# The recurrence's skip made on VectorE and added on GpSimd, in place of four diagonal matmuls for each chunk

## The chip, the cores and the metric

The kernel runs on one core of a Trainium2 chip. The metric is the device time of one execution in microseconds. The engines run side by side and are ordered by semaphores alone: TensorE (PE in the profile, its weight loads PEld), VectorE (DVE), ScalarE (ACT), GpSimd (POOL) and the DMA queues. Everything is float32. A chunk is 128 tokens, a block is 512 tokens, that is four chunks.

## The reference, cut to what matters

The program has three stages on 4096 tokens of width 256. The first one is a graph product followed by a Mamba-2 block, the second a graph product followed by a Mamba-1 block, the third a mixture of experts. Only the first stage's recurrence is touched:

```python
xh, Bmat, Cmat = split(silu(conv(xBC)))          # xh: tokens x 8 heads x 64
xdt    = xh * dt[..., None]
Y_diag = einsum(Cc, Bc, Lmat, xdt)               # inside a chunk
Y_off  = einsum(Cc, prevs, exp(A_cum))           # from the carried state
Y = Y_diag + Y_off + xh * D[:, None]             # the last term is the skip
Y = Y * silu(z)
Y = Y * rsqrt(mean(Y * Y) + EPS) * norm_w
out = Y @ W_out @ W_lin + b_lin                  # W_out @ W_lin is made once ("Wc")
```

`D` has one number for each head. The kernel works in chunks of 128 tokens, which gives the same result.

## The kernel before

The first stage takes eight blocks, numbered 0 to 7. In the period of block b three kinds of work run side by side, and their order on every engine is one list written out by `order_a[b]`; a name in the list lets the generator of that name go one step.

- `product_a(b+2)` ("p" on TensorE, "w" on VectorE): the graph product of a later block. TensorE makes 64 matmuls of 512 columns (L685). Their weights are `exp(...)` of the adjacency matrix: ScalarE (L1659) and VectorE (L1146, L1153, pairs of 128x1024) work on them through six buffers `wgt`. In blocks 6 and 7 TensorE makes the next stage's first product instead (L709), which takes no VectorE work.
- `pre_a(b+1)`: norm, input projection, convolution (L1222, L1225) and silu of the next block. TensorE's step L745 waits for VectorE's L1201, the normalised input `xc`.
- `ssd(b)`: the recurrence. Chunk s has an `inner(s)` and an `outer(s)`. The order is inner(0), inner(1), outer(0), inner(2), outer(1), inner(3), outer(2), outer(3).

For one chunk, `inner(s)` transposes x on TensorE into the PSUM bank X (L785); VectorE makes `xdt` from it (L1251), copies B (L1254) and masks C times B (L1256); GpSimd makes `xdec` (L2190) and, when ScalarE has exponentiated E, multiplies E by the mask (L2195, called M(s) here). `outer(s)` is:

- TensorE: state's part Yo (L807, waits until the state of the chunk before, `hs`, is written by VectorE L1271), new state St (L812), then into bank Y the skip as four matmuls with a 128x128 diagonal matrix of D (L817), and on top of it eight matmuls of 64 columns, the chunk's own part (L823, waits for M(s)).
- GpSimd: `hd(s)`, the decayed state (L2207).
- VectorE: tmp = Yo times decay (L1266), the new state hs = hd + St (L1271), tmp = tmp + Y (L1275), z = tmp times z (L1278). ScalarE then squares z (L1660) into `ms`, and overwrites `tmp` with it, so L1266 of the next chunk waits for that.

After the fourth chunk ScalarE makes `rms`, VectorE scales the four chunks of z (L1288, L1292), and TensorE transposes them (L840, waits for each scaled chunk), multiplies by Wc (L849), and makes the block's norm (L634, L638) and message (L861).

The setup makes `diagD` (L1124) at the start of the program, and at the second pair of message blocks Wc by L875 on TensorE and L1320 on VectorE. `rows` holds three broadcast vectors that one DMA loads (L2127); ScalarE's first exponential waits for it.

Of the kernel before, what the change touches and what calls it, by code (L numbers as in the profile page):

```python
# [148 lines left out]
def build(nc, t):  # L149
    with ExitStack() as ctx:  # L150
# [7 lines left out]
        def sb(c, name, shape, dt=F32):  # L158
            return c.enter_context(nc.sbuf_tensor(name, shape, dt))
# [34 lines left out]
        rows = sb(cA, "rows", [128, NROW])  # L194
        Bbc, dtb, Abc = rows[:, 0:256], rows[:, 256:288], rows[:, 288:296]
        diagD = sb(cA, "diagD", [128, 4, 128])
# [22 lines left out]
        hd = sb(cA, "hd", [64, 512])  # L219
        cA.close()  # L220
# [53 lines left out]
        ring_a, ring_b = Ring(PS[2:5], 6 * NB // 2), Ring(PS[5:8], 6 * NB // 2 + 4)  # L274
# [7 lines left out]
        def message_use(ib, i):  # L282
            if ib % 2:
                return ring_b.use(ib // 2 * 6 + (4 if ib > 1 else 0) + i)
            return ring_a.use(ib // 2 * 6 + i)

        def combined_use(m):
            return ring_b.use(6 + m)

# [134 lines left out]
        def raw_read(g):  # L424
            ib, i = divmod(g - NCH, NQ)
            h, r = divmod(i, NQ // 2)
            if ib == 0:
# [9 lines left out]
                  (S("hd"), 4 * NB), (S("M"), 4 * NB), (S("xdec"), 4 * NB), (S("halo"), NB + 1),  # L437
# [173 lines left out]
        def _(e):  # L611
# [163 lines left out]
            def ssd(ib):  # L775
# [18 lines left out]
                def outer(s):  # L794
# [19 lines left out]
                    w.wait_ge(S("setup"), 5)  # L814
                    w.wait_ge(Y.evac, Y.n - 1)
                    for m in range(4):
                        e.matmul(Y.ps[:, m * 128:(m + 1) * 128], cc[:, m, ts_], diagD[:, m, :], start=m == 0, stop=False,  # L817
                                 skip_group_check=True)
# [267 lines left out]
            def mean_of_bias():  # L1086
                b = end_use(2)
                w.wait_ge(S("b2c"), 1)
# [25 lines left out]
        def _(e):  # L1114
# [11 lines left out]
            def messages(ib):  # L1126
# [8 lines left out]
                w.wait_ge(S("d_rows"), 16)  # L1135
                for s in range(4):
                    b = message_use(ib, 2 + s)
                    w.wait_ge(b.full, b.n)
                    e.tensor_tensor(msg[:, 4 * ib + s, :], b.ps[:, 0:256], Bbc, ALU.add).then_inc(b.evac, 1)
# [97 lines left out]
            def ssd(ib):  # L1237
# [3 lines left out]
                def inner(s):  # L1241
# [8 lines left out]
                    w.wait_ge(S("xdec"), c - 1)  # L1250
                    e.tensor_tensor(heads(xd[:, :]), heads(X.ps[:, :]), dt[:, 8 * s:8 * s + 8, None].broadcast_to([128, 8, 64]),  # L1251
# [7 lines left out]
                def outer(s):  # L1259
# [14 lines left out]
                    w.wait_ge(Yo.evac, Yo.n)  # L1274
                    e.tensor_tensor(tmp[:, :], tmp[:, :], Y.ps[:, :], ALU.add).then_inc(Y.evac, 1)  # L1275
# [289 lines left out]
            def second_matrices():  # L1565
# [9 lines left out]
                e.tensor_scalar(b2[:, 0, :], b2[:, 0, :], tw[:, 0:1], None, ALU.mult).then_inc(S("b2a"), 1)  # L1575
                w.wait_ge(S("b2a"), 1)
# [72 lines left out]
        def _(e):  # L1649
# [14 lines left out]
            w.wait_ge(S("d_rows"), 16)  # L1664
# [458 lines left out]
        def _(e):  # L2123
# [3 lines left out]
            e.dma_start(rows[:, :], t["rows"].broadcast_to([128, NROW])).then_inc(S("d_rows"), 16)  # L2127
# [48 lines left out]
            def ssd(ib):  # L2176
# [22 lines left out]
                def outer(s):  # L2199
# [9 lines left out]
                    yield from [None] * 5  # L2209
# [168 lines left out]
```

## Time and profile before

| | |
|---|---|
| median of three runs | 2359.26 us (2359.06 to 2360.04) |
| span of the profiled execution, first to last instruction | 2358.5 us |
| TensorE busy | 2189.1 us, 93% |
| VectorE busy | 1803.0 us, 76% |
| ScalarE busy | 1566.7 us, 66% |
| GpSimd busy | 1146.6 us, 49% |
| mean granted clock of TensorE | 0.979 |
| first stage, by the timeline | until about 1050 us |
| period of a block in its steady part | 112.38 us (the same L823 group starts at 353.53, 465.91, 578.29, 690.66 and 803.03 us) |

Every float32 matmul stands in the trace as two records, so "x2" is one matmul and "x8" are four. A busy time of TensorE contains the modelled tails of pipelined matmuls; the distance between starts tells what a group takes. In a timeline, "[1.90 <-POOL hd]" is idle time ahead of the instruction, and who ended it. Two instructions merged into one line ("x2") may hold time in which the engine stood still between them.

### The profile page before, as it was taken

Reading aid. Unit: us, or ns where it says so; the run is one execution under the profiler, and the core shown is the slowest. Engines: PE = TensorE matmul, PEld = TensorE weight load, DVE = VectorE, ACT = ScalarE, POOL = GpSimd, SP = SyncE. Lnnn points to the kernel's source line nnn. Section 1 sums busy time; section 2 is a strip of 40 time slices with the busy share of each in tenths; the row PEclk is TensorE's granted clock in tenths of the full one; section 3 lists DMA queues with packets and bytes.
Section 4 is the critical chain, followed back from the end, with each engine's and each line's share of the span. In section 5 each row is a group of like instructions: output and inputs, shape, how many; then the busy total and the mean of one; then the engine's idle time right before and its main releaser. Section 6 shows DMA issues by size and latency. Waiting matters only on the chain.

```text
span 2358.5 us, 26231 instructions
## 1 busy us (share of the span) xinstructions
PE 2189.1 (93%) x8900; PEld 1393.1 (59%) x8900; DVE 1803.0 (76%) x2083; ACT 1566.7 (66%) x2541; POOL 1146.6 (49%) x928
## 2 busy tenths in 40 slices
PE   7999999999999999989999999998999987787998
PEld 4544545555555556456766666676766664444886
DVE  5666767777777765324999998999989998996665
ACT  5577686777686845425676767677676868775444
POOL 2101322222231313213988888888988888890000
PEclk9999999999999999999999999999999999898999
DMA  6243332323232323233323232323323221312121
GB/s 234 72 134 102 108 116 90 125 96 122 87 125 88 119 90 134 83 107 109 131 93 125 90 125 89 117 99 107 117 100 125 90 83 43 117 36 98 36 81 45
DMA packets 117495, 241.22 MB, mean 102 GB/s; under 512 B 8770, under 2 KB 66370, under 8 KB 116978
## 3 DMA queue, kind: packets, MB, share of 16 engines
q1 hardware_dynamic: 108290, 207.14, 26.4%
q0 software_dynamic: 8528, 31.36, 3.8%
q8 instruction: 71, 1.16, 0.2%
q10 hardware_dynamic: 544, 1.05, 0.1%
q14 instruction: 62, 0.51, 0.1%
HBM read 219.20 MB, written 20.32 MB: 102 GB/s over the span
## 4 chain that ended last, share of the span: by engine, by line
PE 65%; ACT 10%; POOL 10%; DVE 10%; issue 5%; DMA 0%; ACTq 0%; DVEq 0%; POOLq 0%
PE ps L685 13%; PE ps L727 10%; POOL dB L2306 6%; PE ps L971 5%; DVE h L1473 3%; PE ps L849 2%; PE ps L823 2%; PE ps L955 2%; POOL acc L2288 2%; PE ps L709 2%; ACT ps L1659 2%; ACT L1657 1%; POOL du L2302 1%; PE ps L755 1%; PE ps L753 1%
## 5 line engine op out<-in xcount | busy, mean ns | idle before, releaser
L1473 DVE TENSOR_TENSOR_SCAN h<-ps,hst,dB 128x512 f32<-128x512 f32 x512 | 636.9, 1270 | 59.0 <-ACT ps L1659 50.5
L2306 POOL TENSOR_TENSOR dB<-du,bc 128x512 f32<-128x512 f32 x512 | 648.0, 1287 | 61.6 <-DVE h L1473 59.1
L685 PE MATMUL ps<-wgt,msg 128*128 128x512 f32 x1024 | 489.0, 598 | 2.1 <-DVE xb L1181 2.1
L1659 ACT ACTIVATE ps<-dt,cols 128x512 f32<-128x512 f32 x512 | 351.9, 692 | 181.1 <-DVE h L1473 178.8
L727 PE MATMUL ps<-raw,msg 128*128 128x256 f32 x1792 | 436.3, 379 | 0.9 <-ACT hb L1659 0.9
L971 PE MATMUL ps<-consts,h 128*128 128x128 f32 x2048 | 318.9, 281 | 70.7 <-DVE acc L1435 38.0
L971 PEld LDWEIGHTS ps<-consts,h 128*128 128x128 f32 x2048 | 251.6, 144 | 224.8 <-DVE acc L1435 73.4
L727 PEld LDWEIGHTS ps<-raw,msg 128*128 128x128 f32 x1792 | 324.0, 190 | 74.1 <-issue 42.1
L685 PEld LDWEIGHTS ps<-wgt,msg 128*128 128x128 f32 x1024 | 190.0, 192 | 206.2 <-issue 204.6
L1659 ACT ACTIVATE wgt<-wgt 128x1024 f32<-128x1024 f32 x256 | 257.9, 1046 | 51.9 <-DVE wgt L1146 50.5
L2288 POOL TENSOR_TENSOR acc<-acc,part 128x512 f32<-128x512 f32 x174 | 226.4, 1301 | 59.7 <-ACT part L1659 58.3
L1146 DVE SCALAR_TENSOR_TENSOR wgt<-wgt 128x1024 f32<-128x1024 f32 x128 | 174.4, 1403 | 54.6 <-ACT wgt L1659 54.6
L1435 DVE SCALAR_TENSOR_TENSOR acc<-ps,Ct,acc 128x512 f32<-128x512 f32 x267 | 193.6, 725 | 5.3 <-PE ps L971 5.2
L1153 DVE SCALAR_TENSOR_TENSOR wgt<-raw,wgt 128x1024 f32<-128x1024 f32 x128 | 167.3, 1348 | 17.9 <-ACT wgt L1659 17.9
L1659 ACT ACTIVATE wgt<-raw 128x1024 f32<-128x1024 f32 x128 | 129.0, 1045 | 24.1 <-PE ps L685 23.9
L2195 POOL TENSOR_TENSOR E<-E,cbm 128x1024 f32<-128x1024 f32 x32 | 81.4, 2545 | 108.4 <-ACT E L1659 108.3
L2226 POOL DMA_DIRECT2D tmp_x<-xb x8 | 5.6, 696 | 254.5 <-DVE xb L1298 254.5
L1659 ACT ACTIVATE part<-ps,Ct 128x512 f32<-128x512 f32 x174 | 117.8, 677 | 1.7 <-PE ps L971 1.5
L2313 POOL TENSOR_TENSOR sq<-sq 128x512 f32<-128x512 f32 x7 | 9.0, 1289 | 207.8 <-ACT sq L1659 207.8
L1660 ACT ACTIVATE tmp<-z 128x512 f32<-128x512 f32 x32 | 20.2, 630 | 130.8 <-DVE z L1278 130.8
L1659 ACT ACTIVATE g<-ps,b 128x512 f32<-128x512 f32 x64 | 43.1, 685 | 84.4 <-PE ps L1052 79.5
L1225 DVE SCALAR_TENSOR_TENSOR cc<-xbc,cols,cc 128x512 f32<-128x512 f32 x120 | 93.6, 780 | 3.1
(320 smaller groups left out, 3589.9 us busy)
## 6 DMA issues: line engine op xcount, KB each, us to landing
raw<-in_adjT SPq DMA_DIRECT2D x256, 512.0 KB, 3.4
bc<-tmp_bc SPq DMA_DIRECT2D x64, 512.0 KB, 4.6
E<-tmp_bc POOLq DMA_DIRECT2D x32, 512.0 KB, 4.1
xb<-in_xT POOLq DMA_DIRECT2D x8, 512.0 KB, 4.1
tmp_x<-xb POOLq DMA_DIRECT2D x8, 512.0 KB, 4.2
x<-tmp_x SPq DMA_DIRECT2D x8, 512.0 KB, 5.8
tmp_x<-x SPq DMA_DIRECT2D x8, 512.0 KB, 4.8
msg<-in_W SPq DMA_DIRECT2D x4, 1024.0 KB, 10.6
```

Source lines behind the costliest of these rows:

```text
L685: x = e.matmul(P[d][:, :], msg[:, j, d * 128:(d + 1) * 128], wgt[g % NW][:, l, :], start=j == 0, stop=j == NJ - 1)
L727: x = e.matmul(P[0][:, 256 * d:256 * d + 256], msg[:, j, d * 128:(d + 1) * 128], quarters(g)[:, l, :], start=j == 0 and d == 0, stop=j == ...
L971: i = e.transpose(b.ps[:, m * 128:(m + 1) * 128], hr[n % 3][:, m, s * 128:(s + 1) * 128], ident)
L1146: e.scalar_tensor_tensor(wgt[i % NW][:, :, :], wgt[i % NW][:, :, :], -2.0, wgt[i % NW][:, :, :], ALU.add, ALU.mult).then_inc(S("q"), 1)
L1153: e.scalar_tensor_tensor(wgt[i % NW][:, :, :], raw[i % 4][:, :, :], 1.0, wgt[i % NW][:, :, :], ALU.is_lt, ALU.mult).then_inc(S("wgt"), 1)
L1225: e.scalar_tensor_tensor(c, xbc[:, m, k:k + TB], col("cw0", 4 * m + k), c, ALU.mult, ALU.add).then_inc(S("conv"), 1)
L1435: e.scalar_tensor_tensor(acc[:, s, :], b.ps[:, :], c, acc[:, s, :], ALU.mult, ALU.add).then_inc(b.evac, 1)
L1473: e.tensor_tensor_scan(hr[n % 3][:, m, :], PS[4 + k % 2].t[:, :], dBr[k % 4][:, :], hst[:, n % 16, m:m + 1], ALU.mult, ALU.add).then_inc(S ...
L1659: return e.activation(out, in_, func, bias=bias, scale=scale)
L2195: e.tensor_tensor(E[c % 3][:, :, :], E[c % 3][:, :, :], cbms[s % 2][:, None, :].broadcast_to([128, 8, 128]), ALU.mult).then_inc(S("M"), 1)
L2288: e.tensor_tensor(acc[:, s, :], acc[:, s, :], part[HANDED[j] % 2][:, :], ALU.add).then_inc(S("summed"), 1)
L2306: e.tensor_tensor(dBr[k % 4][:, :], du[:, m, :], bcr[i % 3][:, n % 2, :], ALU.mult).then_inc(S("dB"), 1)
```

## The change

The skip is no longer part of bank Y. VectorE multiplies x, which is in bank X, by a row of D that stands on every partition (`Drow`), into one of two new buffers `skips`, in `inner(s)` ahead of `xdt`; X is handed back after both. GpSimd, in `outer(s)` two steps behind `hd`, adds tmp (the state's part) to it. VectorE's addition of Y then takes `skips` in place of `tmp`, and waits for GpSimd. The four matmuls L817 are gone, and the eight of L823 each start their own columns.

The setup still makes `diagD`, now in the memory of `skips[0]`; one matmul of ones by diagD (512 columns) and one VectorE copy out of PSUM make `Drow` from it, behind Wc's four steps. That takes a use of a PSUM bank in `ring_b`. `rows` is loaded by two DMAs, the message bias apart, and two waits for it ask for 32 in place of 16. In the third stage a semaphore of its own (`b2a`) is folded into `b2c`; the instructions stay.

```diff
@@ outer, TensorE
-                    w.wait_ge(S("setup"), 5)
                     w.wait_ge(Y.evac, Y.n - 1)
-                    for m in range(4):
-                        e.matmul(Y.ps[:, m * 128:(m + 1) * 128], cc[:, m, ts_], diagD[:, m, :], start=m == 0, stop=False,
-                                 skip_group_check=True)
                     yield
                     w.wait_ge(S("M"), 4 * ib + s + 1)
                     w.wait_ge(X.evac, X.n)
                     for h in range(8):
-                        i = e.matmul(Y.ps[:, h * 64:(h + 1) * 64], Es[:, h, :], xd[:, h * 64:(h + 1) * 64], start=False,
-                                     stop=h == 7, skip_group_check=True)
+                        i = e.matmul(Y.ps[:, h * 64:(h + 1) * 64], Es[:, h, :], xd[:, h * 64:(h + 1) * 64], start=True,
+                                     stop=True)
@@ setup, TensorE (behind the four L875 groups)
+                    b = drow_use()
+                    w.wait_ge(S("setup"), 5)
+                    w.wait_ge(b.evac, b.n - 1)
+                    e.matmul(b.ps[:, :], one, skip0[:, :], start=True, stop=True).then_inc(b.full, 1)
@@ inner, VectorE
+                    if c < 2:
+                        w.wait_ge(drow_use().evac, drow_use().n)
+                    e.tensor_tensor(skips[s % 2][:, :], X.ps[:, :], Drow[:, :], ALU.mult)
                     e.tensor_tensor(heads(xd[:, :]), heads(X.ps[:, :]), dt[:, 8 * s:8 * s + 8, None].broadcast_to([128, 8, 64]),
                                     ALU.mult).then_inc(X.evac, 1)
@@ outer, VectorE
                     w.wait_ge(Y.full, Y.n)
-                    w.wait_ge(Yo.evac, Yo.n)
-                    e.tensor_tensor(tmp[:, :], tmp[:, :], Y.ps[:, :], ALU.add).then_inc(Y.evac, 1)
+                    w.wait_ge(S("skip"), c + 1)
+                    e.tensor_tensor(tmp[:, :], skips[s % 2][:, :], Y.ps[:, :], ALU.add).then_inc(Y.evac, 1)
@@ setup, VectorE (behind the four L1320)
+                    b = drow_use()
+                    w.wait_ge(b.full, b.n)
+                    e.tensor_copy(Drow[:, :], b.ps[:, :]).then_inc(b.evac, 1)
@@ start, GpSimd
-            e.dma_start(rows[:, :], t["rows"].broadcast_to([128, NROW])).then_inc(S("d_rows"), 16)
+            e.dma_start(rows[:, :], t["rows"][:, D:NROW].broadcast_to([128, NROW - D])).then_inc(S("d_rows"), 16)
+            e.dma_start(Bbc[:, :], t["rows"][:, 0:D].broadcast_to([128, D])).then_inc(S("d_rows"), 16)
@@ outer, GpSimd (behind hd)
-                    yield from [None] * 5
+                    yield from (None, None)
+                    Yo = outer_use(ib, s, 0)
+                    w.wait_ge(Yo.evac, Yo.n)
+                    e.tensor_tensor(skips[s % 2][:, :], skips[s % 2][:, :], tmp[:, :], ALU.add).then_inc(S("skip"), 1)
+                    yield from (None, None, None)
```

## Rows read from the trace of the kernel before

**Rows 1.** The page: busy time and share of the span, by engine.
```profile
PE 2189.1 (93%) x8900; PEld 1393.1 (59%) x8900; DVE 1803.0 (76%) x2083; ACT 1566.7 (66%) x2541; POOL 1146.6 (49%) x928
```

**Rows 2.** Busy time in three stretches: each engine, granted clock, DMA share, GB/s.
```profile
380.00:500.00 120.00, 117.76 (x409) 63.26 (x408) 91.07 (x107) 90.64 (x142) 32.39 (x24) 1.00 0.31 103
459.50:517.50 58.00, 57.97 (x235) 33.90 (x235) 47.47 (x58) 39.80 (x67) 19.01 (x13) 1.00 0.34 111
860.00:940.00 80.00, 79.58 (x306) 45.58 (x305) 44.29 (x65) 37.09 (x77) 21.73 (x20) 1.00 0.34 119
```

**Rows 3.** All waits of TensorE between 335 and 785 us: total, times, longest.
```profile
PE ps L634 <- DVE tmp L1303: 4.6, 4, 1.1
PE ps L861 <- DVE z L1312: 4.1, 4, 1.0
```

**Rows 4.** The chain that ended last, 415 to 530 us: start, length, what.
```profile
457.35 0.60 DVE xdt L1251
...
458.35 1.14 DVE xc L1201
...
459.53 1.95 PE ps L745 x16
...
465.02 0.89 PE ps L817 x8
```

**Rows 5.** VectorE in order of time, block 2: start, length, what, idle before.
```profile
459.40 2.35 DVE L1153 SCALAR_TENSOR_TENSOR wgt<-raw,wgt 128x1024 f32<-128x1024 f32 x2
...
468.27 0.68 DVE L1275 TENSOR_TENSOR tmp<-tmp,ps 128x512 f32<-128x512 f32 x1
...
484.90 0.69 DVE L1275 TENSOR_TENSOR tmp<-tmp,ps 128x512 f32<-128x512 f32 x1 [0.65 <-PE ps L823]
...
496.23 4.47 DVE L1153 SCALAR_TENSOR_TENSOR wgt<-raw,wgt 128x1024 f32<-128x1024 f32 x2 [0.22 <-ACT wgt L1659]
500.62 0.67 DVE L1271 TENSOR_TENSOR hs<-hd,ps 64x512 f32<-64x512 f32 x1
502.95 0.69 DVE L1275 TENSOR_TENSOR tmp<-tmp,ps 128x512 f32<-128x512 f32 x1 [1.66 <-PE ps L823]
...
512.49 0.69 DVE L1275 TENSOR_TENSOR tmp<-tmp,ps 128x512 f32<-128x512 f32 x1
...
515.17 0.49 DVE L1288 TENSOR_SCALAR z<-z,rms 128x512 f32<-128x512 f32 x1 [1.26 <-ACT rms L1659]
```

**Rows 6.** GpSimd's plain addition at L2153: ns min/median/max, first and last start.
```profile
L2153 POOL TENSOR_TENSOR rr<-xb x8: 1266/1270/1275, 106.4 to 839.6; 128x512 f32<-128x512 f32 x8
```

**Rows 7.** GpSimd in order of time, the same stretch.
```profile
461.10 2.88 POOL L2195 TENSOR_TENSOR E<-E,cbm 128x1024 f32<-128x1024 f32 x1 [2.02 <-ACT E L1659]
463.94 1.03 POOL L2207 TENSOR_TENSOR hd<-hs,ecd 64x512 f32<-64x512 f32 x1
...
478.21 2.39 POOL L2195 TENSOR_TENSOR E<-E,cbm 128x1024 f32<-128x1024 f32 x1 [5.64 <-ACT E L1659]
...
494.84 2.78 POOL L2195 TENSOR_TENSOR E<-E,cbm 128x1024 f32<-128x1024 f32 x1 [2.79 <-ACT E L1659]
497.60 2.02 POOL L2207 TENSOR_TENSOR hd<-hs,ecd 64x512 f32<-64x512 f32 x1
```

**Rows 8.** TensorE in order of time, the same stretch.
```profile
503.66 1.02 PE L807 MATMUL ps<-hs,cc 128*128 128x512 f32 x2
...
517.50 0.60 PE L840 MATMUL ps<-consts,z 128*128 128x128 f32 x4
```

**Rows 9.** All engines in order of time, block 7.
```profile
998.92 0.68 DVE L1271 TENSOR_TENSOR hs<-hd,ps 64x512 f32<-64x512 f32 x1 [5.02 <-POOL hd L2207]
...
1009.36 1.12 PE L807 MATMUL ps<-hs,cc 128*128 128x512 f32 x2 [0.67 <-DVE hs L1271]
```

**Rows 10.** The chain that ended last, 30 to 130 us.
```profile
37.25 0.48 DVE Wc L1320
```

**Rows 11.** All engines in order of time, the start.
```profile
11.93 1.22 DVE L1130 TENSOR_TENSOR xc<-xb,ps 128x1024 f32<-128x1024 f32 x1 [0.76 <-PE ps L648]
```

More of the change, by code:

```diff
@@ L193, in build @@
         Wc = sb(cA, "Wc", [128, 4, D])
-        rows = sb(cA, "rows", [128, NROW])
-        Bbc, dtb, Abc = rows[:, 0:256], rows[:, 256:288], rows[:, 288:296]
-        diagD = sb(cA, "diagD", [128, 4, 128])
+        rows = sb(cA, "rows", [128, NROW - D])
+        dtb, Abc = rows[:, 0:32], rows[:, 32:40]
+        Drow = sb(cA, "Drow", [128, 512])
         xbs = [sb(cA, f"xb{i}", [128, 2, TB]) for i in range(3)]
@@ L219, in build @@
         hd = sb(cA, "hd", [64, 512])
+        skip0 = sb(cA, "skip0", [128, 512])
+        cM = ExitStack()
+        Bbc = sb(cM, "Bbc", [128, D])
+        cM.close()
+        skips = [skip0, sb(cA, "skip1", [128, 512])]
+        diagD = skip0[:, :].rearrange("p (m c) -> p m c", m=4)
         cA.close()
@@ L271, in build @@
         lane_b = (ccs[0][:, 2:4, :], ccs[0][:, 4:6, :], xdecs[1][:, :])
-        ring_a, ring_b = Ring(PS[2:5], 6 * NB // 2), Ring(PS[5:8], 6 * NB // 2 + 4)
+        ring_a, ring_b = Ring(PS[2:5], 6 * NB // 2), Ring(PS[5:8], 6 * NB // 2 + 5)
         prod = [Ring(PS[0:1], 3 * NB + 1), Ring(PS[1:2], NB + 1)]
@@ L283, in message_use @@
             if ib % 2:
-                return ring_b.use(ib // 2 * 6 + (4 if ib > 1 else 0) + i)
+                return ring_b.use(ib // 2 * 6 + (5 if ib > 1 else 0) + i)
             return ring_a.use(ib // 2 * 6 + i)
@@ L288, in combined_use, with drow_use @@
             return ring_b.use(6 + m)
+        def drow_use():
+            return ring_b.use(10)
         def pre_use(ib, i):
@@ L436, in build @@
         over_a = [(prod[1].use(NB).full, prod[1].use(NB).n), (ssd_use(NB - 1, 27).evac, ssd_use(NB - 1, 27).n), (ssd_use(NB - 1, 31).evac, ssd_use(NB - 1, 31).n),
-                  (S("hd"), 4 * NB), (S("M"), 4 * NB), (S("xdec"), 4 * NB), (S("halo"), NB + 1),
+                  (S("hd"), 4 * NB), (S("M"), 4 * NB), (S("skip"), 4 * NB), (S("xdec"), 4 * NB), (S("halo"), NB + 1),
                   *((S(f"d_x2_{b}"), 16 * len(range(b, NB, 3))) for b in range(3)), (S("d_m2"), 16 * (NB - 2))]
@@ L1087, in mean_of_bias @@
                 b = end_use(2)
-                w.wait_ge(S("b2c"), 1)
+                w.wait_ge(S("b2c"), 2)
                 w.wait_ge(b.evac, b.n - 1)
@@ L1134, in messages @@
                 yield
-                w.wait_ge(S("d_rows"), 16)
+                w.wait_ge(S("d_rows"), 32)
                 for s in range(4):
@@ L1138, in messages @@
                     w.wait_ge(b.full, b.n)
-                    e.tensor_tensor(msg[:, 4 * ib + s, :], b.ps[:, 0:256], Bbc, ALU.add).then_inc(b.evac, 1)
+                    e.tensor_tensor(msg[:, 4 * ib + s, :], b.ps[:, 0:256], Bbc[:, :], ALU.add).then_inc(b.evac, 1)
                     yield
@@ L1574, in second_matrices @@
                 w.wait_ge(b_tw.evac, b_tw.n)
-                e.tensor_scalar(b2[:, 0, :], b2[:, 0, :], tw[:, 0:1], None, ALU.mult).then_inc(S("b2a"), 1)
-                w.wait_ge(S("b2a"), 1)
+                e.tensor_scalar(b2[:, 0, :], b2[:, 0, :], tw[:, 0:1], None, ALU.mult).then_inc(S("b2c"), 1)
+                w.wait_ge(S("b2c"), 1)
                 e.scalar_tensor_tensor(b2c[:, :], b2[:, 1, :], tw[:, 1:2], b2[:, 0, :], ALU.mult, ALU.add).then_inc(S("b2c"), 1)
@@ L1663, in _ @@
             e.dma_start(spots[1], t["xT"][:, :, TB:2 * TB]).then_inc(S("d_x0"), 16)
-            w.wait_ge(S("d_rows"), 16)
+            w.wait_ge(S("d_rows"), 32)
             act(Abc, Abc, ACT.Exp).then_inc(S("Aexp"), 1)
```

## Prediction

> **What bounds the kernel now.** First the page: TensorE is busy for 93% of the span, VectorE for 76% [rows 1]. Shares over three stages say little on one of them, so next comes the busy time by stretch. In the steady part of the first stage TensorE is at 98% with its clock at full speed, VectorE and ScalarE at 76% and GpSimd at 27% (first line) [rows 2]. Then TensorE's waits: over four blocks it waits in two places only, about 1.1 us at L634 and 1.0 us at L861 in each block [rows 3]. Blocks 0 to 5 are thus bound by the length of TensorE's own list, and work taken out of it counts, so long as nothing that TensorE waits for comes too late for the shorter list. That is the question here, since the change gives work to VectorE, which in the same stretch is not far from full: its shares are means, and between L745 and the first L840 of a block (459.5 to 517.5) it is busy for 47.5 of 58 us (second line) [rows 2]. So the third view is the timeline of VectorE and GpSimd over one block (block 2), and the chain of waits across it.
>
> **What is removed.** A group of four L817 takes 0.89 us on the chain [rows 4]; a little of it is the step from one shape of matmul to the next, which stays, so I take 0.86. There are 4 groups in a block, 3.44 us, and 32 in all, 27.5 us. That is the most the change can give.
>
> **What is added on VectorE.** One product a chunk, 32 in all. Its nearest row is L1251, which also reads X in PSUM, with a small second input: it takes 0.60 us on the chain [rows 4]. The second input here is a full tile out of SBUF, as in L1275, which is 0.68 us long with its tail [rows 5]; so 0.61 us each, bounds 0.60 and 0.69. One of the four is free (inner(0) follows a wait for TensorE). The one of inner(1) is not: L1251, L1254, L1256 and L1201 run back to back, and TensorE's L745 starts 0.04 us behind L1201 [rows 4]. TensorE comes there at the same time as before, so it newly waits 0.61 us in each of blocks 0 to 5. From there on the list of TensorE can gain 3.44 - 0.61 = 2.83 us a block at best.
>
> **What is added on GpSimd.** An addition of two 128x512 tiles in SBUF, 1.27 us by L2153 [rows 6] (the multiplication L2207 on 64 partitions takes 1.03, the lower bound) [rows 7]. GpSimd has room for 5.1 us a block, busy for 19 of those 58 us (second line) [rows 2]. What it does to its neighbour matters more. The rows show that the two engines take turns: the pair L1153 at 496.23 takes 4.47 us where the pair at 459.40 takes 2.35 [rows 5], and under it M(3) takes 2.78 and hd(2) 2.02 in place of 2.39 and 1.03 [rows 7]. Reading it as turns: M(3) to 497.6, first half of the pair to 498.7, hd to 499.6, second half to 500.7. That reproduces all three lengths.
>
> The Trainium skill, SBUF — State Buffer, section "Who interferes with whom", says the same as a rule: a VectorE instruction with two SBUF inputs and a GpSimd instruction that reads SBUF exclude each other for the whole instruction, and whoever starts first holds the port. It speaks against this change, since the new addition reads SBUF twice; it also says that the product and L1275, with one input in PSUM, are not hit. If the new addition blocked nothing, step 5 below would be 1.3 us better and step 4 up to 1.3: 8 to 15 us in all. The trace agrees with the rule by the three lengths above.
>
> **A walk through block 2 with the new work.** Times are those of the old trace, delays are against it.
> 1. L1201 ends at 460.0, 0.6 late. Behind it the pair L1153, M(1) and hd(0) exclude each other: 2.27 (2.35 less its tail) + 2.36 + 1.03 us, to 465.7, where hd(0) ended at 464.97 [rows 5, 7]. L1275(0) comes at about 468.97, 0.7 late.
> 2. ScalarE is busy without a gap from the square of z(0) until 480.5, and hands the 0.7 us on to M(2) and hd(1) [rows 7].
> 3. The new addition of chunk 1 waits for VectorE's pair and runs from 484.3 to 485.6; L1275(1), which waits for it, is 0.7 late as well (before 484.90) [rows 5].
> 4. A second product (chunk 3) adds 0.61 us ahead of the pair L1146, M(3), L1225, hd(2), the pair L1153 and the new addition, again in turns. L1271(2), before 500.62 to 501.24 [rows 5], ends at 502.8 or 504.1: if VectorE's second L1225 gets ahead of M(3) the former, if M(3) does the latter. TensorE needs it for L807(3), before at 503.66 [rows 8] and now wanted at 503.66 + 0.61 - 3 x 0.86 = 501.7. It waits 1 to 2.4 us.
> 5. L1275(2) was at 502.95, L1275(3) 9.54 us later, with VectorE busy without a gap ahead of it [rows 5]. The last addition falls on the pair L1146 and adds 1.27. From 503.5 or 504.1: L1275(3) at 514.3 or 514.9, where it was at 512.49. So z(3), `rms` and the first scaled chunk are d = 1.8 or 2.4 us late.
> 6. The scaled chunk was ready at 515.57 (start 515.17, 0.40 to the next) [rows 5] and TensorE took it at 517.50 [rows 8]: 1.93 us of slack. The gain of a block is the lesser of 2.83 and 1.93 - d: +0.15 or -0.5 us.
>
> Behind L840 VectorE is loaded lightly (4 to 5 of 8 us), waits for TensorE, and hands nothing on.
>
> **Other terms.** Block 6: no adjacency work on VectorE, busy 55%, TensorE at 99.5% (third line) [rows 2]; no pair to take turns with, so 4 x 0.86 = 3.4 us are gained (bounds 2 and 3.4). Block 7: TensorE waits for L1271(2) at L807(3) [rows 9], at the end of a chain from L823(0) over E, M and hd. The groups of chunks 0 and 3 count, those between only lengthen that wait: 1.7 us, less 0.6 since L1275(1), which followed L1271 of 998.92 at once [rows 9], now waits 1.27 us behind hd: 1.1 gained (bounds 0 and 3.4). Setup: a matmul (0.86 us) and a copy (0.5, L1320 takes 0.48 [rows 10]) behind the last Wc, which is on the chain: 1.1 lost (bounds 0 and 1.5). The two DMAs for `rows`: one more issue on GpSimd's queue ahead of ScalarE's first exponential, for which VectorE's L1122 waits; VectorE still rested 0.76 us behind that setup [rows 11], so 0 (bounds 0 and 0.5). The third stage's semaphore: 0. Nothing else of TensorE's order moves, and the banks X, given back 0.61 us later, are next written 10 us or more later.
>
> **Sum**, against the span 2358.5 us. Six blocks between +0.15 and -0.5 us are +0.9 to -3.0, middle -1.0; block 6 gives 3.4, block 7 gives 1.1, the setup takes 1.1: 2.4 us gained. As the two answers of step 4 weigh about the same and the two delays of step 1 were both taken at their full size, I round the gain up to 3.0. The median of the runs is 2359.26, 0.8 above the span; the gain goes off it: 2356.3 us.
>
> **The rivals.**
> - *TensorE's list stays the bound (0.25).* The new additions fall into VectorE's rests (10.5 us between L745 and L840) [rows 2] and the exclusion costs nothing new; d stays under -0.9. For it speaks that TensorE comes earlier at each place where VectorE waits for it (0.65 and 1.66 us) [rows 5]. Against it the waits that are not TensorE's (hd, ScalarE's wgt and squares). Six blocks at 2.0 to 2.83, and the other terms: 15.4 to 20.4 us, so 2339 to 2344.
> - *VectorE and GpSimd become the bound and cost more than the matmuls (0.2).* One mechanism: each of the four additions holds up a pair between L745 and L840 (5.1 us), and three products (1.8 us) lie on the same line, less what its rests take (about 3). d is then 3.9, and a block loses 2.0; six lose 12, less 3.4 from the other terms: 2367.9. It decides from d = 1.93 + 0.57 = 2.5 on, where six blocks lose what the rest gains; between, 2360 to 2368.
> - *The change does not act as told (0.05):* the eight L823 of 64 columns, each now a group of its own, or the bank's shift in the setup take back what L817 gave. L823 has the same loads and columns, so I expect it at 0.216 us each as before; then about 2359.
>
> **How the numbers follow.** Forecast with its own range, 2352 to 2361: 0.5. Less than 0.2% (4.7 us) can hardly be told from no change in this kernel. Faster by more: the first rival 0.25 and a third of the forecast's case, 0.17: 0.42. Slower by more (above 2364): most of the second rival and a little of the forecast's: 0.19. Within: 0.39. For eight times in ten the range takes in the first rival down to 2341 and the second up to 2365.
>
> **What would show it.** TensorE's busy time less by about 27 us, no L817, 32 more VectorE instructions of 0.69 us and 32 on GpSimd of 1.27 (up to 2.4 where they wait). The period of a block, 112.38 us now: 112.2 to 112.9 if I am right, 109.6 to 110.4 by the first rival, 114 by the second. New waits of TensorE: L745 for L1201 with 0.6 us a block, L807 for L1271 with 1 to 2.4, L840 for L1288. If L807 and L840 show no wait, step 4 or 5 is wrong. If L1225 or L1153 are not lengthened where the new addition runs, the turns are read wrongly.

## The result, and the profile after

The changed kernel takes 2373.45 us (median of four runs, 2370.09 to 2378.2). The kernel before, on the same chip, took 2359.16 (2358.82 to 2360.04). The ratio is 1.0061 with a 95% interval of 1.0049 to 1.0073: slower by 14 us, where 2356.3 was forecast and 2365 was the upper end of the range. The profiled execution is the fastest of the four, 2370.09 us with a span of 2367.9, so the trace explains 9.4 us of span out of the 14.

First the page's line by engine, which answers to [rows 1].

```profile
span 2367.9 us, 25802 instructions
PE 2172.7 (92%) x8646; PEld 1366.4 (58%) x8646; DVE 1864.7 (79%) x2116; ACT 1566.7 (66%) x2541; POOL 1190.5 (50%) x961
```

The matmuls are gone: 254 records fewer (two for each of the 128, less the two of the new matmul in the setup), TensorE busy for 16.4 us less. But VectorE is busy for 61.7 us more, where 32 products of 0.69 us are 22. So about 40 us of VectorE's time is no new work but old work made longer.

The second view is the busy time by block. A block here runs from one L754 (before: L745) of the list to the next. The columns are those of [rows 2].

```profile
348.66:462.76 114.10, 109.02 (x353) 56.10 (x353) 93.41 (x105) 84.01 (x132) 33.03 (x26) 0.99 0.32 106
462.76:577.73 114.97, 108.75 (x352) 56.18 (x353) 93.55 (x105) 84.12 (x132) 33.34 (x26) 0.99 0.33 106
```

The period was 112.38 us and is 114.10 to 114.13, or 114.95 to 114.97 in two of the blocks (the second line is one of them), in which TensorE's clock falls behind L754; the last section has this. Followed by the starts of these blocks, blocks 0 to 5 cost 12.7 us, blocks 6 and 7 give back 2.9, and the setup gains 0.3, together the 9.4.

TensorE's waits from 335 to 785 us, as in [rows 3]:

```profile
PE ps L816 <- DVE hs L1283: 6.7, 4, 1.8
PE ps L643 <- DVE tmp L1315: 4.6, 4, 1.1
PE ps L845 <- DVE z L1300: 3.7, 2, 1.8
PE ps L866 <- DVE z L1324: 3.1, 3, 1.0
PE ps L754 <- DVE xc L1210: 2.7, 4, 0.7
PE ps L762 <- ACT z L1674: 0.7, 2, 0.3
```

Two of these lines are those of before (L643 and L866). Of the four new ones L816, L845 and L754 are the three waits that the walk had named; the small one at L762, for ScalarE, it had not. What had to be explained is why they are worth 1.7 us a block more than the matmuls.

Last VectorE and GpSimd in order of time, from L1155 of chunk 1 to the first scaled chunk of block 2, as [rows 5, 7] (start, length, what, idle before).

```profile
483.15 6.05 DVE L1155 SCALAR_TENSOR_TENSOR wgt<-wgt 128x1024 f32<-128x1024 f32 x2 [0.45 <-ACT wgt L1674]
...
507.49 0.67 DVE L1287 TENSOR_TENSOR tmp<-skip,ps 128x512 f32<-128x512 f32 x1
508.19 1.03 DVE L1290 TENSOR_TENSOR z<-tmp,z 128x512 f32<-128x512 f32 x1
...
510.96 4.46 DVE L1155 SCALAR_TENSOR_TENSOR wgt<-wgt 128x1024 f32<-128x1024 f32 x2 [0.18 <-ACT wgt L1674]
...
519.45 0.68 DVE L1287 TENSOR_TENSOR tmp<-skip,ps 128x512 f32<-128x512 f32 x1
...
522.12 0.49 DVE L1300 TENSOR_SCALAR z<-z,rms 128x512 f32<-128x512 f32 x1 [1.26 <-ACT rms L1674]
```

```profile
484.87 2.02 POOL L2223 TENSOR_TENSOR hd<-hs,ecd 64x512 f32<-64x512 f32 x1
486.86 1.26 POOL L2228 TENSOR_TENSOR skip<-skip,tmp 128x512 f32<-128x512 f32 x1
...
507.64 1.04 POOL L2223 TENSOR_TENSOR hd<-hs,ecd 64x512 f32<-64x512 f32 x1 [2.90 <-DVE hs L1283]
510.85 1.27 POOL L2228 TENSOR_TENSOR skip<-skip,tmp 128x512 f32<-128x512 f32 x1 [2.18 <-DVE tmp L1278]
512.08 2.26 POOL L2169 TENSOR_TENSOR rr<-xb 128x512 f32<-128x512 f32 x1
```

In the kernel before, the same two pairs of VectorE, and the half sum of GpSimd:

```profile
479.10 4.56 DVE L1146 SCALAR_TENSOR_TENSOR wgt<-wgt 128x1024 f32<-128x1024 f32 x2 [0.73 <-ACT wgt L1659]
...
506.09 2.36 DVE L1146 SCALAR_TENSOR_TENSOR wgt<-wgt 128x1024 f32<-128x1024 f32 x2 [0.19 <-ACT wgt L1659]
```

```profile
502.48 1.27 POOL L2153 TENSOR_TENSOR rr<-xb 128x512 f32<-128x512 f32 x1
```

The pair L1155 of chunk 1 is stretched to 6.05 us. Alone such a pair takes 2.35, and before the change it took 4.56 here, with M and hd on it; now M, hd and the addition L2228, all three of GpSimd, fall on it. The addition starts 0.03 us before hd's record ends, and the pair's second half waits through both. The last pair at 510.96 is stretched to 4.46 by two instructions: the addition, and behind it L2169, the half sum of the block after next. L2169 is in both kernels; before, it ran right behind the last hd, ahead of this pair. From Y's addition (L1287) of chunk 2 to that of chunk 3 it is now 11.96 us; before it was 9.54, and the walk had 10.81. Of the 2.4 us more, 2.1 are this pair; the other 0.3 are z's product L1290, which takes 1.03 us in place of 0.69 beside hd of chunk 3. It does so without any addition too (in the kernels below that leave them out), since the chunk's matmuls now end earlier.

### The profile page after: what moved, and what is told of

It reads as the page before. It is cut to its first block, busy times and chain, and to the rows that moved or that the text cites. A ratio compares the mean times of both kernels' runs of the same rounds, so it can differ in the third digit from the quotient of the medians.

```text
span 2367.9 us, 25802 instructions
## 1 busy us (share of the span) xinstructions
PE 2172.7 (92%) x8646; PEld 1366.4 (58%) x8646; DVE 1864.7 (79%) x2116; ACT 1566.7 (66%) x2541; POOL 1190.5 (50%) x961
## 4 chain that ended last, share of the span: by engine, by line
PE 48%; DVE 15%; ACT 15%; POOL 13%; issue 8%; DMA 1%; DVEq 0%; ACTq 0%; POOLq 0%
PE ps L736 9%; PE ps L694 7%; POOL dB L2326 6%; PE ps L980 5%; DVE h L1488 3%; ACT wgt L1674 3%; ACT E L1674 3%; PE ps L854 2%; DVE wgt L1162 2%; DVE wgt L1155 2%; PE ps L964 2%; POOL acc L2308 2%; ACT L1672 2%; ACT ps L1674 2%; POOL E L2211 1%
## 5 line engine op out<-in xcount | busy, mean ns | idle before, releaser
L1155 DVE SCALAR_TENSOR_TENSOR wgt<-wgt 128x1024 f32<-128x1024 f32 x128 | 197.3, 1581 | 43.7 <-ACT wgt L1674 43.7
L1162 DVE SCALAR_TENSOR_TENSOR wgt<-raw,wgt 128x1024 f32<-128x1024 f32 x128 | 173.8, 1398 | 15.8 <-ACT wgt L1674 15.4
L1234 DVE SCALAR_TENSOR_TENSOR cc<-xbc,cols,cc 128x512 f32<-128x512 f32 x120 | 105.6, 880 | 3.1
```

What stands on the lines that cost most here:

```text
L1155: e.scalar_tensor_tensor(wgt[i % NW][:, :, :], wgt[i % NW][:, :, :], -2.0, wgt[i % NW][:, :, :], ALU.add, ALU.mult).then_inc(S("q"), 1)
L1162: e.scalar_tensor_tensor(wgt[i % NW][:, :, :], raw[i % 4][:, :, :], 1.0, wgt[i % NW][:, :, :], ALU.is_lt, ALU.mult).then_inc(S("wgt"), 1)
L1234: e.scalar_tensor_tensor(c, xbc[:, m, k:k + TB], col("cw0", 4 * m + k), c, ALU.mult, ALU.add).then_inc(S("conv"), 1)
```

## The experiments

The theories that the expectations name by letters are in short: A, the additions take turns with VectorE's pairs, and the chain to the scaled chunk becomes late; B, the time without L817 isn't freed at all; C, the product ahead of L754, with the clock that falls behind its wait; D, the order in which the addition gets its turn; E, the half sum moved behind the last addition. Periods are from one L754 to the next, of blocks in which TensorE's clock doesn't fall behind L754.

| kernel | us | ratio to before (95%) | period |
|---|---|---|---|
| before | 2359.2 | 1 | 112.38 |
| changed | 2373.45 | 1.0061 (1.0049 to 1.0073) | 114.1 |
| no product, no addition | 2337.61 | 0.9914 (0.9897 to 0.9930) | 109.13 |
| products alone | 2343.54 | 0.9940 (0.9924 to 0.9957) | 109.6 |
| additions alone | 2366.90 | 1.0035 (1.0024 to 1.0047) | 113.4 |
| two memsets for each addition | 2348.61 | 0.9960 (0.9946 to 0.9974) | 110.2 |

**Products and additions taken out, then one of the two at a time.**

```diff
-                    w.wait_ge(S("skip"), c + 1)
+                    w.wait_ge(Yo.evac, Yo.n)
-                    e.tensor_tensor(skips[s % 2][:, :], skips[s % 2][:, :], tmp[:, :], ALU.add).then_inc(S("skip"), 1)
+                    if c < 2:       # the product, in the first and third kernel only
```

> The changed kernel without the skip work that was added: the 32 GpSimd additions are left out and 30 of the 32 VectorE products (those of chunks 0 and 1 of block 0 stay); the diagonal matmuls stay gone, so the skip is missing from the result. Theory A (VectorE and GpSimd, taking turns, have become the bound of blocks 0 to 5, and the matmuls' time was really freed): TensorE's list is the bound again, a block takes 112.38 - 3.5 = 108.9 us, block 6 gains 3.4, block 7 1.7, the setup costs 1.1: 2334 to 2337. Theory B (the eight matmuls of 64 columns as groups of their own, or the shifted bank, cost what the diagonal ones gave): about as the changed kernel, 2365 to 2375.

> The changed kernel without GpSimd's 32 additions: VectorE adds the product to Y, so the state's part is missing from the result; VectorE waits for its own L1278 in place of GpSimd. Theory A with the addition as main cause: only the products are left, TensorE waits 0.6 us a block at L754 and VectorE's late chain 0 to 1 us more, so a block takes 109.6 to 111 us: 2338 to 2348. If the products are the main cause: 2362 to 2370.

> The changed kernel without 30 of VectorE's 32 products (chunks 0 and 1 of block 0 keep theirs); GpSimd's additions stay, on stale numbers. Theory A: the wait at L754 is gone (0.6 us a block) and 1.2 us of VectorE's line with it, the turns of the additions stay: a block takes 111.5 to 113 us, 2350 to 2362. If the products are the main cause: 2338 to 2348.

Without either, 2337.61 us, 0.6 above the range expected: the time of the 128 matmuls is really freed, 21.6 us of it, 3.25 in a block (3.44 by the prediction), and TensorE's waits are those of before. This rules out B. With the products it is 2343.54, 5.9 more and as expected. With the additions alone it is 2366.90, 29.3 more, outside the 2350 to 2362 expected: the additions alone cost more than the matmuls gave. TensorE's waits of that kernel over four blocks:

```profile
PE ps L845 <- DVE z L1301: 7.3, 4, 1.8
PE ps L816 <- DVE hs L1284: 6.2, 4, 1.6
PE ps L643 <- DVE tmp L1316: 4.6, 4, 1.1
PE ps L866 <- DVE z L1325: 4.1, 4, 1.0
PE ps L762 <- ACT z L1675: 1.8, 4, 0.5
```

The two add up: 5.9 and 29.3 are 35.2, and both together cost 35.8. More than four fifths of it is the additions.

**Is it the turns?** The addition is replaced by two memsets of the same tile: the same place on GpSimd, the same wait, 2 x 0.52 us in place of 1.26, but nothing is read from SBUF.

```diff
-                    e.tensor_tensor(skips[s % 2][:, :], skips[s % 2][:, :], tmp[:, :], ALU.add).then_inc(S("skip"), 1)
+                    e.memset(skips[s % 2][:, :], 0.0).then_inc(S("skip"), 1)
+                    w.wait_ge(S("skip"), 2 * (4 * ib + s) + 1)
+                    e.memset(skips[s % 2][:, :], 0.0).then_inc(S("skip"), 1)
```

> The changed kernel with GpSimd's addition replaced by two memsets of the skip tile, one behind the other: about as long on GpSimd (0.54 us each, some 1.15 in all), in the same place, with VectorE waiting for them in the same way, but reading nothing from SBUF. The skip and the state's part are missing from the result. Theory A1 (turns between VectorE's two SBUF inputs and GpSimd's reads): no pair is lengthened by them, a block takes 109.6 to 111.5: 2340 to 2350. Theory A2 (the wait for GpSimd, or GpSimd's own time): little change, 2366 to 2374.

2348.61 us, and of a block:

```profile
344.24:454.48 110.24, 107.00 (x352) 55.59 (x352) 89.79 (x105) 84.02 (x132) 31.28 (x30) 1.00 0.34 110
```

Of the 30 us between products alone and the changed kernel, 25 are gone, with the instruction, its wait and its place still there. VectorE is busy for 89.79 us of the block, not 93.41, and its pair of chunk 1 takes 4.53 us, as before the change. So the cost is in the main the reading beside VectorE. The wait for GpSimd and the chain through it are at most the 5 us that are left, and these also hold the half sum, which stands behind the memsets as it did behind the additions.

**The other way round: the same work put into the kernel before.** First an addition on GpSimd behind each hd, which nothing reads; then one product a block, that of chunk 1.

```diff
+                    e.tensor_tensor(scr[:, :], cin, cin, ALU.add).then_inc(S("skip"), 1)
```

> The kernel before, diagonal matmuls and all, with one more thing: GpSimd adds two 128x512 tiles of constants into a scratch tile, where the changed kernel has its addition (behind hd, after VectorE's L1266), and nobody reads the scratch or waits for it. Theory A1 (the addition costs because VectorE's pairs with two SBUF inputs and GpSimd's reads take turns, whoever waits for the sum): VectorE's L1146 and L1153 pairs get longer by 1.27 us where it falls on them, the first L840 waits for VectorE, and a block takes 113 to 115 us: 2362 to 2372. Theory A2 (it costs because VectorE waits for the sum): no change, 2358 to 2361, a block 112.4.

```diff
+                    if s == 1:
+                        e.tensor_tensor(scr[:, 0:512], X.ps[:, 0:512], Wc[:, 0:2, :].rearrange("p k d -> p (k d)")[:, 0:512], ALU.mult)
```

> The kernel before with one more VectorE product a block, X in PSUM by Wc into a scratch tile, in inner(1), ahead of xdt; nobody reads it. Theory C1: TensorE waits 0.6 us at L745 in each of blocks 0 to 5, and in some of them the granted clock falls behind it to 0.5 for 3 us, which costs another 1.5 us there, since TensorE is the bound: a block takes 113.0 or 114.5, 2363 to 2372. Without the clock: 113.0 in every block, 2362.5 to 2363.5.

The additions cost next to nothing: 2360.25 us, ratio 1.0004 (0.9994 to 1.0013), which is under what A1 gave them (2362 to 2372), and 112.50 us a block. Only block 0 takes 1.9 us longer, with the clock at half of its level for some 3 us near its start. The trace shows two reasons. First, the dummy lost its turn to the pair:

```profile
482.34 2.02 POOL L2208 TENSOR_TENSOR hd<-hs,ecd 64x512 f32<-64x512 f32 x1
484.32 2.01 POOL L2216 TENSOR_TENSOR scr<-consts 128x512 f32<-128x512 f32 x1
```

It took 2.01 us, and VectorE's pair of chunk 1 stayed at 4.52. Why it lost its turn is open: it starts 0.03 us before hd's record ends, as the real addition does, and the semaphore that it alone waits for, the dummy's of the chunk before, had long been counted up. It reads one tile twice, which takes 1.04 us where VectorE is not in the way, and not 1.26. Second, what the last dummy did, with the half sum behind it (a last pair of 4.23 us where it was 2.36, the scaled chunk 1.85 us later), fell into the slack that the kernel before has. The prediction read that slack as 1.93 us. It is 1.79, since TensorE starts L845 0.14 us behind the scaled chunk even when it waits for it, and 1.85 against 1.79 fits the 0.1 us a block that is lost here. The changed kernel has spent the slack with what it takes out of TensorE's list. So nearly the same instructions cost about 1 us in one kernel and 29 in the other by that slack and these turns; how much is due to each, and to the shorter dummy, isn't shown.

The kernel with the product takes 2363.35 us (2361.47 to 2367.56), as expected for a clock that doesn't fall. In the profiled execution, one of the short ones, the product costs 0.60 us a block (112.98, from 112.38), with a wait of 0.67 at L746 in blocks 1 to 5, as the prediction had it. But the ten executions fall into two groups, six at 2361.5 to 2363.8 and four at 2366.3 to 2367.6. The clock may fall in the four; there is no trace of them.

**The product ahead of L754.** Once it is left out in chunk 1, once moved behind xc.

```diff
+                    if s != 1 or c == 1:
                         e.tensor_tensor(skips[s % 2][:, :], X.ps[:, :], Drow[:, :], ALU.mult)
```

> The changed kernel without the product of chunk 1 of blocks 1 to 7, the one ahead of L1210 that L754 waits for. Theory C (the new wait of 0.67 us at L754 lets TensorE's granted clock fall for some 3 us in about half of the blocks): no wait at L754, no stretch with a clock under 0.9 behind it in blocks 0 to 5; a block takes 113.5 in all of them, and the spread between runs (8 us in the changed kernel) falls under 1 us: 2366 to 2369. Theory A alone: 0.6 us a block less, 2369 to 2370, with the clock falling as before.

```diff
-                    e.tensor_tensor(skips[s % 2][:, :], X.ps[:, :], Drow[:, :], ALU.mult)
+                    if s == 1:      # two steps later, behind bn, cbm and xc
+                        e.tensor_tensor(skips[s % 2][:, :], X.ps[:, :], Drow[:, :], ALU.mult).then_inc(X.evac, 1)
```

> The changed kernel with the product of chunk 1 moved behind L1210, and xdt made ahead of the product in the others; two counts of the semaphore bn stand for xdt and the copy. The result is complete. The wait of 0.67 us at L754 goes, the turns stay: a block takes 113.6 us, as without that product: 2365 to 2371. If the late product costs the same as the early one (VectorE's line is full behind it as well): 2371 to 2375.

2370.44 (2365.49 to 2371.54) and 2368.93 us (2366.63 to 2370.49): the first is a little above what both theories gave it, the second within its range. In both the wait at L754 is gone and TensorE waits for the scaled chunk instead: 113.63 and 113.89 us a block. So the product is worth 0.2 to 0.5 us a block, not its 0.67. The part of C which laid the spread of the runs on this wait falls: with no wait there the runs still spread over 6 and 4 us. The clock doesn't fall behind L754 in either, but in some of the blocks it now falls behind the wait at L816, where it costs nothing (113.62 us a block with it, 113.63 without).

**The whole skip on VectorE.**

```diff
-                    e.tensor_tensor(tmp[:, :], skips[s % 2][:, :], Y.ps[:, :], ALU.add).then_inc(Y.evac, 1)
+                    e.tensor_tensor(tmp[:, :], tmp[:, :], Y.ps[:, :], ALU.add).then_inc(Y.evac, 1)
+                    e.tensor_tensor(tmp[:, :], skips[s % 2][:, :], tmp[:, :], ALU.add).then_inc(S("ysum"), 1)
```

> The changed kernel with the addition moved to VectorE: tmp = tmp + Y out of PSUM as before the change, then tmp = skip + tmp from SBUF, 0.61 us more of VectorE for each chunk in place of 1.27 us of GpSimd. The result is complete. Theory A1: VectorE's line gets 4 x 0.61 us a block longer than without any addition, which is less than the turns cost; a block takes 110.5 to 112.5, so 2346 to 2358. If VectorE's total load is what counts and not the turns (84% of the block against 82%): no better than the changed kernel, 2368 to 2376.

2374.86 us, where 2346 to 2358 was expected. TensorE's wait at L845 grows to 2.1 us. The one block without a fall of the clock takes 113.0 us, 1.1 less than in the changed kernel; the others take 113.95, with the fall behind L754, or 114.70, with the fall behind the wait at L845. VectorE's own line from L754 to the scaled chunk can't take four more instructions either: the scaled chunk comes 3.9 us later than with the products alone. Over the whole kernel the addition costs about the same on VectorE as on GpSimd.

**Which addition gets ahead of which half.** In the changed kernel the addition stands right behind hd in GpSimd's queue. With one more wait it is let go only when hd has ended.

```diff
+                    w.wait_ge(S("hd"), 4 * ib + s + 1)
                     e.tensor_tensor(skips[s % 2][:, :], skips[s % 2][:, :], tmp[:, :], ALU.add).then_inc(S("skip"), 1)
```

> The changed kernel, where GpSimd's addition waits for the semaphore of the hd that GpSimd issued just before it; nothing else. In the changed kernel the addition of chunks 1 and 2 runs in 1.25 us right behind hd, and VectorE's pair, with M, hd and the addition going first, takes 5.75 us; in the kernel before with a dummy addition that waited for a semaphore of its own the addition took 2.01 us and the pair 4.5. Theory D (an instruction of GpSimd that stands ready behind another one goes ahead of VectorE's waiting half, one that has still to wait lets it through): pairs of 4.5 us again in chunks 1 and 2, L1283 of chunk 2 about 1.2 us earlier, a block takes 112.5 to 113.4: 2364 to 2369. Rival (the order of turns comes from the phase of the two lists): pairs stay at 5.75 us, 2371 to 2375.

```profile
482.47 4.52 DVE L1155 SCALAR_TENSOR_TENSOR wgt<-wgt 128x1024 f32<-128x1024 f32 x2 [1.59 <-ACT wgt L1674]
```

```profile
483.89 2.02 POOL L2223 TENSOR_TENSOR hd<-hs,ecd 64x512 f32<-64x512 f32 x1
486.05 2.07 POOL L2229 TENSOR_TENSOR skip<-skip,tmp 128x512 f32<-128x512 f32 x1
```

With the wait for hd the order is as D has it: the pair takes 4.52 us where it took 5.75 (6.05 in the block above), and now the addition is the one that waits, 2.07 us for 1.26. L1283 of chunk 1 comes 1.0 us earlier. But chunk 2 keeps only 0.4 of it, the period is 113.69, and the median, 2372.36 us where 2364 to 2369 was expected, can't be told from that of the changed kernel. The trace has blocks 0 to 5 at 675.0 us where they took 679.6, and all that follows 8.7 us longer, with the clock at half of its level four times between 940 and 1055 us, in the changed kernel once there. The effect of the wait is real and small.

**The half sum.** It is put ahead of the last addition, where it stood, behind the last hd.

```diff
+                    if s == 3 and ib + 2 < NB:
+                        w.wait_ge(S("hd"), 4 * ib + 4)
+                        halves(ib + 2)
                     Yo = outer_use(ib, s, 0)
                     w.wait_ge(Yo.evac, Yo.n)
```

> The changed kernel with GpSimd's L2169 (the half sum rr, 1.27 us, which stood behind hd of chunk 3 and now stands behind that chunk's addition) issued between the two, as early as before the change; nothing else. Theory E (L2169, held up by the addition, now falls on VectorE's pair L1155 together with it: 4.45 us in place of 2.36 for the pair, where the addition alone would add 1.27): the pair takes 3.6, L1287 of chunk 3 comes 0.8 us earlier, a block takes 113.2 to 113.4 in place of 114.1, 2368 to 2370. Rival (the pair waits for the addition alone, or loses the time by its own second half): 114.1 as before.

The same two places in this kernel, VectorE, then GpSimd:

```profile
507.93 3.39 DVE L1155 SCALAR_TENSOR_TENSOR wgt<-wgt 128x1024 f32<-128x1024 f32 x2 [0.18 <-ACT wgt L1674]
```

```profile
504.61 1.04 POOL L2223 TENSOR_TENSOR hd<-hs,ecd 64x512 f32<-64x512 f32 x1 [2.89 <-DVE hs L1283]
505.73 1.60 POOL L2169 TENSOR_TENSOR rr<-xb 128x512 f32<-128x512 f32 x1
507.83 1.28 POOL L2231 TENSOR_TENSOR skip<-skip,tmp 128x512 f32<-128x512 f32 x1 [0.49 <-DVE tmp L1278]
```

L2169 now runs beside instructions that it hardly holds up, the pair takes 3.39 us, the scaled chunk comes 1.06 us earlier, and the period is 113.04: 1.07 less, for one instruction moved past another, and more than the 0.7 to 0.9 expected. The median is 2369.11 us (2365.3 to 2370.69), within the 2368 to 2370 expected.

**All three mends, and the change where there is slack.** The late product, the wait for hd and the half sum first, in one kernel; and, in another, the new way for chunk 0 alone (and chunk 2 of the last two blocks), with diagonal matmuls for the rest.

```diff
+def NEW(ib, s):
+    return s == 0 or s == 2 and ib >= NB - 2
```

> All three single edits together, with a complete result: product of chunk 1 behind L1210, addition waiting for hd, L2169 ahead of the last addition. If the account of the loss is complete (0.2 to 0.6 us a block for the product's place, 0.4 for the turns, 0.8 for L2169), a block takes 112.3 to 112.9, level with the kernel before: 2356 to 2363. If they overlap on the same line: 113 to 113.5, 2363 to 2368.

> The new path for chunk 0 of every block and for chunk 2 of blocks 6 and 7 only; all others keep the diagonal matmuls (diagD has memory of its own, one skip tile, the bias lies where it is). The result is complete. By the event times, chunk 0's product is free (VectorE waits there for L794 anyway) and its addition costs VectorE 0.4 us, which L840's slack of 1.9 us hides; TensorE's list is 0.86 us shorter in each block and another 0.86 in blocks 6 and 7. A block takes 111.5 us; 8 x 0.86 + 2 x 0.86 less 0 to 1.1 for the setup: 2350 to 2353. If any addition costs its 1.27 us on the bound line, 2357 to 2361.

The three mends take 2357.23 us (2355.16 to 2358.32, ratio 0.9992, 0.9982 to 1.0001), 16 us less than the changed kernel: they take back all that it lost, and leave it level with the kernel before. That is within the 2356 to 2363 expected, but the block of 111.74 us is under the 112.3 to 112.9: together they take 2.4 us off a block, and one by one 0.2, 0.4 and 1.1. Why they give more together wasn't looked into. TensorE still waits 1.2 us at L845 and 1.2 at L762 in each block.

The kernel with chunk 0 alone takes 2355.61 us (2352.22 to 2357.77), ratio 0.9983 (0.9974 to 0.9992), and is the fastest complete one, though it misses the 2350 to 2353 expected. Its waits are those of [rows 3], without a new one, and its block

```profile
347.27:458.75 111.48, 109.25 (x376) 58.42 (x376) 84.29 (x102) 84.02 (x132) 28.84 (x23) 1.00 0.33 109
```

is 0.90 us shorter: one group of four matmuls, 0.86 by the prediction. What is missing lies elsewhere: in the profiled execution, the slowest of the eleven, the start up to block 0 is 1.0 us longer, blocks 6 and 7 give 1.0 and not 3.4, and the stages behind, whose instructions are the same, take 2.4 us more.

## Why the prediction was wrong

The form of the sum held. A block gains the lesser of what the list gives and 1.93 - d. TensorE's wait at L754 is 0.67 us. The scaled chunk, by the profile of after, comes 58.49 us behind L754 where it was 55.64, and L754 itself is 0.60 us later: d = 3.45, where 1.8 or 2.4 was forecast. By the formula a block loses 1.52, and 1.66 with the slack of 1.79 that the experiments give; it loses 1.73. The step that failed is the size of d, above all in step 5, and by the prediction's own rule the second rival decides from 2.5 on. That rival had the period (114) right; I gave it 0.2. Its time of 2367.9 us is under all four executions, 2370.09 at the least. That it came so near is in part luck: its d of 3.9 holds four additions and three products and no half sum, and 1.07 of the 3.45 are the half sum.

- *Step 1*, and the wait at L754: right, 0.67 us for 0.61, and L1287(0) 0.9 us late for 0.7.
- *Step 2*: ScalarE's share wasn't followed by itself, and isn't shown.
- *Step 3* failed. I let the addition wait until VectorE's pair had ended. It stood ready behind hd and went ahead of the pair's second half, so L1287(1) is 1.4 us late, not 0.7.
- *Step 4* came out at the second of its two answers. L1283(2) is 2.8 us late, TensorE waits 1.5 to 1.8 us at L816 (1 to 2.4 forecast), and L1287(2) is 1.06 us late, within the 0.55 to 1.15 given.
- *Step 5* is the one that decided. Between L1287(2) and L1287(3) it added 1.27 us for the addition alone, and the trace has 2.41: 1.03 for the addition (the last pair takes 3.39 us with the half sum moved back, 2.36 before), 1.07 for the half sum L2169 and 0.34 for L1290 beside hd of chunk 3. The walk looked at the VectorE instruction under the new addition and not at what stands behind it in GpSimd's queue. Moving L2169 back took its 1.07 away. Over six blocks that is 6.4 us, about half of the error.
- *Step 6*: the middle of six blocks was put between d of 1.8 and 2.4, at -1.0 us. Without the half sum d is 2.4, its upper answer, and a block loses 0.66 us (113.04), 0.5 below that middle: 3 us.
- *The clock* was not in the sum. Blocks 2 and 4 take 0.85 us longer by it (below), and block 5 about 0.5: about 2 us over all.
- *What was removed*: the matmuls gave 3.25 us a block, not 3.44. It doesn't count here, since TensorE waits for the scaled chunk.
- *Blocks 6 and 7* give back 2.9 us, not 4.5: TensorE waits 2.4 us in block 6 for L1283(2), which stands behind L1278 and the convolution, a wait that the walk didn't look for.
- *The setup* costs nothing, for 1.1 forecast: block 0's L754 starts 0.33 us earlier than before. But one execution can't tell: in that of before the clock falls at 134.6 us and in that of after it doesn't, and in the other kernels with the new setup the same L754 starts at 233.8 to 236.3 us. That it fits the bound of 0 may be luck.

The terms are 6.4 + 3 + 2 + 1.6 - 1.4 = 11.6, and the rounding of the forecast, which was upwards by 0.6, makes 12.2, against 2367.9 - 2355.5 = 12.4 us of span. The rest of the distance to the median is the spread of the runs. The profiled one is the fastest of four, and the others lie 3.3 to 8.1 us above it; no trace shows where. All of these terms are read from single executions, so that they add up to the error within 0.2 us is in part luck.

Of the signs: 128 L817 gone, products at 0.69 us and additions at 1.26 were as told. TensorE's busy time fell by 16.4 and not 27, though without the additions and products it fell by 25.8. In part a busy record holds time at the lower clock (the two of L762 at 394.05 take 1.91 us for 1.02); the rest wasn't followed. "Up to 2.4 where they wait" was wrong for the addition in the changed kernel, and telling: the additions didn't wait (mean 1.26), so the pairs did.

## What to carry to other kernels

Price an instruction moved to GpSimd by what it does to the VectorE instructions of two SBUF inputs beside it, and then do the same for every instruction queued behind it on GpSimd, since these move too. Time taken out of the bound engine's list counts only up to the slack of the next chain: measure that slack first (1.8 us here, for 3.25 of savings), and spend the change only on the parts that it covers, as chunk 0 did. Nearly the same work put into the old kernel as a dummy can cost nothing and still be the cost of the new one, since the old one has the slack.

## What the runs showed of the hardware

**Who gets the next turn.** The addition, ready behind hd, goes ahead of VectorE's waiting instruction in chunks 1 and 2 of blocks 0 to 5 (in chunk 1 the pair takes 5.75 us, the addition 1.25). Let go only by the semaphore at hd's end, it lets VectorE in first (pair 4.52, addition 2.07). To be ready isn't enough, though. In both kernels hd of chunk 1 starts 0.04 us before M's record ends, and yet the first half of the pair comes in between (hd takes 2.02 us for 1.03). In the same way the dummy behind hd let in the second half (2.01 for 1.04). What decides stays open. The Trainium skill, SBUF — State Buffer, section "Who interferes with whom", says that whoever starts first holds the port. The runs agree with that, and show both orders where both are waiting at once. The section also has it that a GpSimd instruction which only writes SBUF doesn't contend with VectorE. The runs agree: memsets in the additions' place cost 0.6 us a block over the products alone, where the additions cost 4.5.

**TensorE's clock behind a short wait.** In the changed kernel the same wait of 0.67 us stands ahead of L754 in blocks 1 to 5. In blocks 1 and 3 it leaves the clock at its full level (2.4 GHz), and in blocks 2, 4 and 5 the clock falls to the lower one (1.2 GHz) for about 3 us. In blocks 1 and 3 it falls instead behind the wait of 1.8 us at L816, in no block at both places. The stretch behind L754 in block 1, the one behind L816 in block 1, and the one behind L754 in block 2, with the columns of [rows 2]:

```profile
349.90:353.00 3.10, 3.10 (x13) 1.79 (x13) 3.10 (x2) 1.54 (x2) 3.10 (x2) 1.00 0.55 169
390.00:397.00 7.00, 5.22 (x8) 1.88 (x8) 5.92 (x7) 2.62 (x4) 2.14 (x2) 0.76 0.49 152
464.50:467.50 3.00, 3.00 (x6) 1.35 (x7) 3.00 (x3) 1.24 (x3) 3.00 (x2) 0.56 0.61 175
```

What the engine did before L754's two stretches was the same: matmuls of 512 columns, the wait, eight of 8 columns. Behind L816 the fall costs nothing, since it takes the place of the wait at L845: that wait stands in blocks 2 and 4 alone of the four in the list above, and blocks 1 and 3 take 114.1 us, as block 0 does without any fall. Behind L754 it costs the changed kernel 0.85 us. Where TensorE is the bound it costs 1.5 us, as in the kernel with the products alone:

```profile
456.01:567.12 111.11, 108.27 (x353) 56.39 (x353) 89.43 (x105) 84.13 (x132) 26.95 (x22) 0.98 0.34 109
567.12:676.73 109.61, 106.76 (x352) 55.73 (x352) 88.67 (x105) 84.04 (x132) 27.48 (x22) 1.00 0.34 111
```

In the kernel before with a product added the same wait stood in five blocks of the profiled execution and the clock fell in none. What decides it stays open.

**Where executions differ.** The kernel with the half sum moved back runs the same instructions as the changed kernel from block 6 on. Here is the stretch from block 6 to the second stage's first scan, and that from there to its last scan, in the changed kernel and then in that one:

```profile
914.16:1116.37 202.21, 185.01 (x670) 108.02 (x669) 77.79 (x116) 82.92 (x170) 55.38 (x50) 0.99 0.31 95
1116.37:2135.80 1019.43, 924.96 (x4459) 659.45 (x4457) 942.95 (x972) 734.83 (x1260) 894.75 (x713) 0.97 0.30 99
```

```profile
906.68:1112.79 206.11, 187.70 (x670) 108.61 (x669) 77.81 (x116) 82.83 (x170) 55.25 (x50) 0.98 0.30 94
1112.79:2134.58 1021.79, 925.53 (x4459) 660.83 (x4457) 943.15 (x971) 734.61 (x1260) 894.53 (x713) 0.97 0.30 99
```

It takes 3.9 and 2.4 us more for them, with the mean clock at 0.98 and not 0.99 in the first. Its blocks 0 to 5 take 7.5 us less, and the two profiled spans are the same, 2367.9 us. So executions can differ by several us where the work doesn't, and a single edit is read better from its blocks than from one execution's time. Whether the wide spread of the changed kernel's runs lies there too stays open, since it has one trace: with the product of chunk 1 left out they spread over 6 us, with it over 8.
